# Start of the second phase of a fused network kernel: rows moved inside SBUF in eight transfers, the last mixed tile in halves, the weight sums divided

## What is computed

```python
def ffn0(x):              # both operands rounded to float8 by one scale for the whole tensor
    amax = max(abs(x)); inv = amax / 448
    return (fp8(x / inv) @ fp8(w.T / w_inv)) * inv * w_inv + bias
mixed = einsum('boi,bih->boh', agg_w, x) + agg_b     # agg_w, agg_b from a small network of cond
x = x + ffn0(mixed)
conv = grouped_conv1d(x, weight, taps=9, groups=4) + ctx + fside   # over the 1024 positions
x = x + conv @ dequantised(W_q).T + bias
```

## Time and profile before

| | |
|---|---|
| median of 3 runs | 534.8 us (534.0 to 535.83) |
| profiled execution, its time | 535.84 us |
| its span, first to last instruction | 534.0 us |
| mean granted TensorE clock | 0.99 |
| TensorE busy in matmuls | 512.7 us (96%) |
| VectorE, ScalarE, GpSimd busy | 411.8, 245.6, 56.4 us |

### The profile page before, as it was taken

How to read it: one execution, slowest core, us unless ns; L and a number is a source line. 1 busy time by engine, 2 the same in 40 slices (tenths; PEclk the granted TensorE clock), 3 DMA queues, 4 the chain that set the end, 5 groups by cost and what they waited for, 6 DMA issues and landing times.

```text
span 534.0 us, 9541 instructions
## 1 busy us (share of the span) xinstructions
PE 512.7 (96%) x3526; PEld 286.5 (54%) x3526; DVE 411.8 (77%) x518; ACT 245.6 (46%) x286; POOL 56.4 (11%) x59
## 2 busy tenths in 40 slices
PE   4999999869999999999999999999999999999997
PEld 3644444336555555555555555555555555555563
DVE  4789999884888777777777777777777777777652
ACT  3488897654544444444444444444444444442310
POOL 6257775000000000000000000000000000000000
PEclk9999999889999999999999999999999999999999
DMA  6999491144666655656665655665555555566632
GB/s 190 398 390 401 148 354 61 44 154 126 182 197 202 188 179 178 178 178 178 180 180 181 185 186 185 186 180 178 178 178 178 178 178 178 180 185 188 198 120 79
DMA packets 86347, 101.28 MB, mean 190 GB/s; under 512 B 34156, under 2 KB 67694, under 8 KB 86334
## 3 DMA queue, kind: packets, MB, share of 16 engines
q1 hardware_dynamic: 85770, 100.89, 59.3%
q10 hardware_dynamic: 372, 0.20, 0.1%
q0 software_dynamic: 192, 0.02, 0.0%
HBM read 59.47 MB, written 33.82 MB: 175 GB/s over the span
## 4 chain that ended last, share of the span: by engine, by line
PE 82%; DVE 10%; POOL 2%; issue 2%; DMA 1%; ACT 1%; DVEq 0%; POOLq 0%; ACTq 0%
PE pair L1107 41%; PE pair L1085 19%; PE pair L1097 16%; DVE stat L759 5%; PE pair L995 2%; PE pair L1075 1%; DVE work L691 1%; PE pair L983 1%; DVE work L774 1%; DMA work<-split_rows 1%; DVE work L694 1%; DVE Y L774 1%; POOL work L436 1%; POOL Y L449 1%; POOL fixed L469 1%
## 5 line engine op out<-in xcount | busy, mean ns | idle before, releaser
L1107 PE MATMUL pair<-f1T,work 128*128 128x512 f16 x1024 | 231.0, 379 | 0.0
L1107 PEld LDWEIGHTS pair<-f1T,work 128*128 128x128 f16 x1024 | 98.9, 98 | 113.5
L580 ACT ACTIVATE work<-Y,consts 128x1024 bf16 (+1 forms) x29 | 33.3, 1148 | 186.9 <-DVE work L848 186.9
L867 DVE TENSOR_TENSOR work<-Y,work 128x512 f16<-128x512 f16 (+1 forms) x64 | 71.1, 1118 | 46.4 <-ACT work L609 45.2
L1085 PE MATMUL pair<-f0T,work 128*128 128x512 bf16 x464 | 104.9, 379 | 0.0
L1097 PEld LDWEIGHTS pair<-taps,work 128*128 128x128 f16 x1536 | 90.2, 99 | 9.5 <-issue 2.2
L1097 PE MATMUL pair<-taps,work 128*128 128x128 f16 x1536 | 92.7, 221 | 1.9 <-DMA work<-split_rows 1.9
L880 DVE TENSOR_TENSOR Y<-pair,Y 128x512 f32 (+1 forms) x64 | 44.0, 687 | 43.9 <-PE pair L1107 43.9
L609 ACT CAST work<-Y 128x512 f16 (+1 forms) x64 | 69.6, 1138 | 15.6 <-DVE Y L857 15.6
L1085 PEld LDWEIGHTS pair<-f0T,work 128*128 128x128 bf16 x464 | 45.4, 98 | 54.7
L995 PE MATMUL pair<-Y,work 128*128 128x512 f32 x128 | 62.7, 625 | 1.1 <-ACT Y L553 0.8
(11 more groups left out here) (149 smaller groups left out, 234.7 us busy)
## 6 DMA issues: line engine op xcount, KB each, us to landing
Y<-in_x_dram SPq DMA_DIRECT2D x64, 512.0 KB, 3.8
split_rows<-work SPq DMA_DIRECT2D x32, 520.0 KB, 2.6
work<-split_rows SPq DMA_DIRECT2D x32, 520.0 KB, 3.9
out_dram<-Y SPq DMA_DIRECT2D x31, 512.0 KB, 3.7
Y<-in_L_ffn_weight_dram SPq DMA_DIRECT2D x8, 512.0 KB, 5.9
Y<-in_L_ffn_W_q_dram SPq DMA_DIRECT2D x5, 512.0 KB, 14.0
work<-in_L_ffn_W_q_dram SPq DMA_DIRECT2D x3, 512.0 KB, 15.3
out_dram<-Y SPq DMA_DIRECT2D x2, 256.0 KB, 2.0
```

The source lines that it names most:

```text
L867: nc.vector.tensor_tensor(split[:, r, s, 1], v[:, r, :], split[:, r, s, 0], ALU.subtract)\
L1107: last = mm(ps[2 + h][:, :], y1s[n][:, e, k, :], f1T[:, k, h * H:(h + 1) * H], start=False, stop=(e == 1 and k == KT - 1), skip_group_chec ...
```

## The change

For tiles 0 and 1, `turn` is replaced by transfers within SBUF. For each of the eight groups one DMA takes sixteen partitions of `split` (4160 bytes each) straight to 128 partitions of `convin` (520 bytes each). SP issues groups 0 and 1 of each half b, and the GpSimd queue groups 2 and 3. The convolution waits for each half by itself, on `moved_sp[b]` and `moved_pool[b]`. For tile 1 the moves wait for conv(0)'s half b, and `hi(1)` waits for the moves of tile 0. From tile 2 on the way over DRAM stays, with its counts shifted.

The last mixed tile is stored and searched in halves. Three of the eight products of `weight_sums(0)` go between the transpose of the exchange and its broadcast. `fixed_parts` falls into a fixed and a sum part, placed between other work. Tile 2's transposes use PSUM banks 6 and 7, and are written as h = 0 and h = 1. On VectorE `first_quantise(2)` goes ahead of `residual0(1)`. ScalarE's loop has its first two steps written out.

```diff
@@ -172,6 +172,7 @@
...
         groups += [(25, 2), (27, 2), (29, 1), (30, 1), (31, 1)]
+        groups[-1:] = [(31, 0), (31, 1)]
         NGRP = len(groups)
@@ -273,6 +274,8 @@
...
         lo_done = sem("lo_done")
+        moved_sp = [sem(f"moved_sp{b}") for b in range(NB)]
+        moved_pool = [sem(f"moved_pool{b}") for b in range(NB)]
         split_out = sem("split_out")
@@ -295,6 +298,12 @@
...
             return turn_order.index((kind, n))
+        def split_row(g):
+            return split[g * CG:(g + 1) * CG].rearrange("p r s e -> p (r s e)")
+        def conv_row(g):
+            return convin[:, g].rearrange("p s e -> p (s e)")
@@ -379,7 +388,7 @@
...
             def turn(t, n, conv_read):
-                both, back = held(sp, 2 * t + 2), held(sp, 16 * t + 16)
+                both, back = held(sp, 2 * t + 2), held(sp, 16 * t - 16)
                 if conv_read is not None:
@@ -393,10 +402,19 @@
...
                 load_x(t, t % 2)
-            turn(0, 0, None)
+            def move(t):
+                sp.wait_ge(lo_done, 2 * t + 2)
+                for b in range(NB):
+                    if t:
+                        sp.wait_ge(conv_done, b + 1)
+                    for g in (b * G, b * G + 1):
+                        sp.dma_start(conv_row(g), split_row(g)).then_inc(moved_sp[b], 16)
+            move(0)
             sp.wait_ge(first_q, 6)
             load_x(2, 0)
-            turn(1, 1, 2)
+            move(1)
             sp.wait_ge(f0_done, 4)
@@ -503,6 +521,14 @@
...
+            for t in range(2):
+                pool.wait_ge(lo_done, 2 * t + 2)
+                for b in range(NB):
+                    if t:
+                        pool.wait_ge(conv_done, b + 1)
+                    for g in (b * G + 2, b * G + 3):
+                        pool.dma_start(conv_row(g), split_row(g)).then_inc(moved_pool[b], 16)
@@ -549,9 +575,11 @@
...
-                act.wait_ge(mixed, t + 1)
-                nc.scalar.activation(slot(t), pair[t % 2][:, :], ACT.Identity, bias=aggcol[:, t:t + 1])\
-                    .then_inc(mixed_ev, 1)
+                for h in range(2 if t == T - 1 else 1):
+                    c = slice(h * H, (h + 1) * H) if t == T - 1 else slice(0, L)
+                    act.wait_ge(mixed, t + 1 + h)
+                    nc.scalar.activation(slot(t)[:, c], pair[t % 2][:, c], ACT.Identity, bias=aggcol[:, t:t + 1])\
+                        .then_inc(mixed_ev, 1)
@@ -591,7 +619,7 @@
...
-                pb = ps[4 + h][:, 0:H // 2].bitcast(bf16).rearrange("p (k m) -> p k m", k=KT // 2)
+                pb = ps[(6 if t == 2 else 4) + h][:, 0:H // 2].bitcast(bf16).rearrange("p (k m) -> p k m", k=KT // 2)
                 act.wait_ge(q_turned, 2 * t + h + 1)
@@ -603,8 +631,12 @@
...
                 for h in range(2):
-                    if h == 0:
-                        act.wait_ge(split_out, 16 * t)
+                    if h == 0 and isinstance(t, int) and t < 3:
+                        for b in range(NB if t else 0):
+                            act.wait_ge(moved_sp[b], 32 * t)
+                            act.wait_ge(moved_pool[b], 32 * t)
+                    elif h == 0:
+                        act.wait_ge(split_out, 16 * t - 32)
                     r = slice(4 * h, 4 * h + 4)
@@ -674,11 +706,17 @@
...
             scaled(3)
-            with act.Fori(2, T - 2 - 1, 2) as i:
+            def loop_step(t, n):
+                scaled(t + 2, n)
+                hi(t)
+                yhi(t - 1, 1 - n)
+            loop_step(2, 0)
+            loop_step(3, 1)
+            with act.Fori(4, T - 2 - 1, 2) as i:
                 for n in range(2):
-                    scaled(i + n + 2, n)
-                    hi(i + n)
-                    yhi(i + n - 1, 1 - n)
+                    loop_step(i + n, n)
             hi(T - 2)
@@ -755,8 +793,13 @@
...
                 t, k = groups[n]
-                dve.wait_ge(mixed_ev, t + k)
-                nc.vector.tensor_reduce(stat[:, n:n + 1], slot(t, k), AX.X, ALU.max,
+                if t < T - 1:
+                    dve.wait_ge(mixed_ev, t + k)
+                    part = slot(t, k)
+                else:
+                    dve.wait_ge(mixed_ev, T + k)
+                    part = slot(t)[:, k * H:(k + 1) * H]
+                nc.vector.tensor_reduce(stat[:, n:n + 1], part, AX.X, ALU.max,
                                         apply_absolute_value=True).then_inc(mixed_red, 1)
@@ -896,8 +939,8 @@
...
             lo(0)
+            first_quantise(2)
             residual0(1, 1, 16)
-            first_quantise(2)
             dve.wait_ge(fixed_ev, 4)
@@ -994,10 +1037,11 @@
...
                               start=True, stop=True)
+                    if h or t == T - 1:
+                        last.then_inc(mixed, 1)
                     if t == 1 and h == 0:
...
                         nc.tensor.transpose(ps[7][0:1, 0:P], w_part, ident[:, :]).then_inc(w_pe, 1)
-                last.then_inc(mixed, 1)
@@ -1050,17 +1094,18 @@
...
                     turned1(turns1[t])
-            def turned_first_q(t):
-                for h in range(2):
-                    pb = ps[4 + h][:, 0:H // 2].bitcast(bf16)
-                    pe.wait_ge(first_q, 2 * t + h + 1)
-                    if t:
-                        pe.wait_ge(qT_in[1 - t % 2], 8 * h + 8)
-                    for k in range(4):
-                        at = (4 * h + k) * P
-                        last = nc.tensor.transpose(pb[:, k * P:(k + 1) * P], qn[t % 2][:, at:at + P], ident_b)
-                    last.then_inc(q_turned, 1)
+            def turned_first_q(t, h):
+                pb = ps[(6 if t == 2 else 4) + h][:, 0:H // 2].bitcast(bf16)
+                pe.wait_ge(first_q, 2 * t + h + 1)
+                if t == 1:
+                    pe.wait_ge(qT_in[0], 8 * h + 8)
+                if t == 2:
+                    pe.wait_ge(fixed_ev, 2 * h + 2)
+                for k in range(4):
+                    at = (4 * h + k) * P
+                    last = nc.tensor.transpose(pb[:, k * P:(k + 1) * P], qn[t % 2][:, at:at + P], ident_b)
+                last.then_inc(q_turned, 1)
@@ -1087,8 +1132,12 @@
...
             def conv(t, first=False):
-                pe.wait_ge(split_in, 16 * t + 16)
+                if not (isinstance(t, int) and t < 2):
+                    pe.wait_ge(split_in, 16 * t - 16)
                 for b in range(NB):
+                    if isinstance(t, int) and t < 2:
+                        pe.wait_ge(moved_sp[b], 32 * t + 32)
+                        pe.wait_ge(moved_pool[b], 32 * t + 32)
                     if not first:
@@ -1108,43 +1157,54 @@
...
-            def weight_sums(h):
+            def weight_sums(h, ks):
                 c = slice(h * H, (h + 1) * H)
-                for k in range(KT):
+                for k in ks:
                     last = mm(ps[h][0:NS, :], windowc[:, 3 * (R8 - 1 - k):3 * (R8 - 1 - k) + NS], f1T[:, k, c],
                               start=(k == 0), stop=(k == KT - 1))
-                last.then_inc(shifted_mm, 1)
-            def fixed_parts(h):
-                c = slice(h * H, (h + 1) * H)
+                if ks[-1] == KT - 1:
+                    last.then_inc(shifted_mm, 1)
+            def fixed_part(h):
                 pe.wait_ge(shifted_ev, h + 1)
-                mm(ps[2 + h][:, :], combT[:, 0:P], shifted[:, c], start=True, stop=True).then_inc(fixed_mm, 1)
-                mm(ps[6 + h][:, :], combT[:, P:2 * P], shifted[:, c], start=True, stop=True).then_inc(wsum_mm, 1)
+                mm(ps[2 + h][:, :], combT[:, 0:P], shifted[:, h * H:(h + 1) * H], start=True, stop=True)\
+                    .then_inc(fixed_mm, 1)
+            def wsum_part(h):
+                mm(ps[6 + h][:, :], combT[:, P:2 * P], shifted[:, h * H:(h + 1) * H], start=True, stop=True)\
+                    .then_inc(wsum_mm, 1)
...
             pe.wait_ge(mixed_ev, T - 1)
-            weight_sums(0)
+            weight_sums(0, range(0, 5))
             pe.wait_ge(mixed_red, NGRP + 1)
             nc.tensor.transpose(ps[7][0:1, 0:P], part_max, ident[:, :]).then_inc(x_pe, 1)
+            weight_sums(0, range(5, KT))
             pe.wait_ge(mixed_red, NGRP + 2)
             mm(ps[7][:, 128:129], ones, x_all, start=True, stop=True).then_inc(x_pe, 1)
-            weight_sums(1)
+            weight_sums(1, range(KT))
             pe.wait_ge(tapsum_made, 1)
             pe.wait_ge(ld["b0"], 32)
-            pe.wait_ge(mixed_ev, T)
-            fixed_parts(0)
-            turned_first_q(0)
+            pe.wait_ge(mixed_ev, T + 1)
+            fixed_part(0)
+            turned_first_q(0, 0)
+            wsum_part(0)
+            turned_first_q(0, 1)
             first_ffn0(0, 0, 0)
-            turned_first_q(1)
+            turned_first_q(1, 0)
+            turned_first_q(1, 1)
+            fixed_part(1)
             first_ffn0(1, 1, 0)
-            fixed_parts(1)
-            turned_first_q(2)
+            pe.wait_ge(x_step, 4)
```

(4 more changed lines are left out.)

## The result

The changed kernel takes 533.88 us (median of 20 runs, 532.73 to 535.26) against 534.89 us for the kernel before, also over 20 runs (533.67 to 536.34). The ratio is 0.9978, with a 95% interval of 0.9968 to 0.9987. That is 1.0 us gained where 3.85 were forecast: the right sign, but within the 0.3% that I had called no change, and above the top of the range (533.4).

The account below looks back on a forecast made before the run. TensorE, busy for 96% of the span and alone from 123.16 us on, bounds the kernel, so only an earlier start gains. Terms -0.2 - 3.45 - 0.2 = -3.85 us take the 534.8 median to 531.0, range 528.9 to 533.4.

Parts of the forecast that it names:

- Last tile in halves: Tile 31's reduction ahead of the exchange: gain 0.37 us, 0.2 given back by three products before the broadcast, net -0.2.
- Fixed part 1 moved: Ahead of the first layer of tile 1: that layer ends 0.4 us late, which costs nothing.
- What is late next: Before conv(0): tile 2's transposes, not the moves, set its start, at 115.1 instead of 118.56, -3.45 us.
- The moves: Behind lo(0): 2.1 us from issue to landing, half 0 there at 114.5 and half 1 at 115.6, before conv(0) needs them.
- My second rival: Moves of tile 0: sixteen partitions feed a transfer slowly, conv(0) starts 2.8 us earlier, 531.7 us; chance 0.10.
- conv(0): The first convolution: takes 4.4 us instead of 4.60 as the clock falls soon after its start, -0.2; bounds 2.68 and 5.4.
- The third rival: Half 0's moves: GpSimd's descriptors wait for VectorE, conv(0) gains only 1.5 us, 533.0 to 533.2 us; chance 0.16.
- GpSimd's transfers didn't run one after the other: Slower rival at conv(1): GpSimd's transfers run in series, 538.6 us if each takes 2.5 us; chance 0.10.
- The clock didn't stay high: Rival at conv(0): the clock stays high and it takes 2.68 us, 529.2 us in all; chance 0.18.

Follow-up runs that it names:

- experiment 4: The changed kernel with all eight products of weight_sums(0) ahead of the exchange: 532.93 us, ratio 0.9948 to the kernel before.
- Experiments 2: The changed kernel with SP moving groups 0 and 2 of each half and GpSimd 1 and 3: 531.22 us, ratio 0.9941 to the kernel before.
- 5: The changed kernel with half 0's four moves on GpSimd's queue and half 1's on SP's: 533.09 us, ratio 0.9969 to the kernel before.
- 8: The changed kernel with all eight moves on SP's queue and none on GpSimd's: 532.54 us in a single run.
- Experiment 3: The changed kernel with 14 idle products into a free PSUM bank ahead of conv(0): 531.76 us, ratio 0.9926 to the kernel before.

## Why the prediction was wrong

**Last tile in halves: right.** Forecast -0.37 and +0.2, net -0.2; measured -0.53 and +0.31, net -0.22. That the net fits so well is partly luck, as both parts came out larger: a half took 0.60 us and not 0.68, and the broadcast slipped by the most that I had allowed. The three products cost what they last beyond the 0.37 us gap, as experiment 4 shows from the other side.

**Fixed part 1 moved: right.** It costs nothing. The first layer of tile 1 ends near 110.1, and residual0(1) comes at 112.4.

**What is late next: half right.** Tile 2's transposes stand where the forecast put them (3.25 us after lo(0) against 3.26). first_quantise(2) took 2.89 us beside four GpSimd issues, 2.88 without them. But they don't set the start of conv(0).

**The moves: the step that failed.** I let half 0 land 2.64 us after lo(0), and it took 5.4. The price of one transfer was nearly right (2.1 forecast, 2.3 and 2.5 measured alone). Wrong was to price eight as one plus the issues ahead of it. First, SP's issue of this shape takes 0.6 us and not 0.34; I had read that price from a transfer of another shape. That alone is 0.3 us for the second one. Second, and more, transfers of two queues at once held each other up, to 2.7 to 4.7 us. My second rival came nearest to the mechanism, and its data phase was about right (4.8 us for eight; here the DMA engines worked on them for 4.2, from 111.0 to 115.2), but it let half 0 finish in half of that. It doesn't: half 1's transfers run beside half 0's, and SP's second one, which half 0 needs, landed after 4.7. Experiments 2, 5 and 8 each thin the crowd in another way and bring conv(0) to 4.6, 5.0 and 4.8 us.

**conv(0): the second step that failed**, -0.2 forecast and +0.7 measured. I had counted on a gap of 2 us ahead of conv(0). It was 2.3 behind the last transposes and 3.7 with only 0.4 us of work in it, the clock fell before conv(0), and it ran low almost to its end. My upper bound of 5.4 was right. The term hung on the moves. Whether the clock would have held with conv(0) at 3.3 us, no run shows: the earliest start, 4.6 us after lo(0), had the clock low from 113.5 as well. Experiment 3 shows its size, 2.4 us.

With the two terms as measured my sum reads -0.2 - 1.2 + 0.7 = -0.7, against -1.0 in the medians.

**Two sums.** By its own terms the lower end of my range is 529.0, not 528.9. The third rival with the sum's other terms is 532.9, not 533.0 to 533.2, which would put the upper end near 533.1. Neither changes that 533.9 lies outside.

**The rivals.** GpSimd's descriptors didn't wait for VectorE: its four issues took 2.13 us together, 0.53 each, all of them beside VectorE's first_quantise(2). The rule of the Trainium skill that I had named there (page "SBUF — State Buffer", section "SBUF: two separate sides") changed nothing here. It speaks of VectorE's two-port modes, and no row shows in which mode these operations ran. GpSimd's transfers didn't run one after the other either. The clock didn't stay high.

**Reading a single profile.** The profiled executions differ by 2.6 us, and 1.5 of it is the first layer of tile 0, which the change doesn't touch. Taken as the change's own, it would have seemed to confirm most of my sum.

**Open.** Why half 0 of eight well dealt moves needs 4.6 us, and all eight 6.5, where one takes 2.5 wasn't separated further: neither the order within a queue nor the size of a transfer was varied alone, and with this dealing tile 2's load was also issued 1.2 us sooner (112.60 against 113.81), beside the last moves. That the instruction packet delays the load is read from two kernels that have both, and wasn't tried alone.

## What to carry to other kernels

Price a crowd of transfers as a crowd: take issue and landing from a transfer of the same shape, run one alone and then the whole set, and try dealing those that run at the same time to partitions 16 or 64 apart instead of 32 (here 0.9 and 0.5 us for the first half, nothing for the last transfer at 16). Before TensorE's start is moved forward, look at what the gap ahead of it does to the clock; here idle products in the gap (2.4 us) were worth more than the shorter way (1.2 us). And where executions fall into groups by mean granted clock, compare within a group before a microsecond is given to an edit, and look in a profile which low stretches make up the group, as the edit may have removed one of them.

## What the runs showed of the hardware

- A move of 65 KB from 16 to 128 partitions within SBUF landed after 2.5 us on SP and 2.3 on GpSimd, one of the same size from 128 to 128 after 1.9. SP's issue took 0.6 to 0.68 us for the narrow shape and 0.55 for the wide one.
- Two queues at once, reading 32 partitions apart: SP's second landing 4.5 to 4.8 us in five profiles (3.6 in a sixth, where the queues started 0.6 us apart), SP's issues up to 1.23 us. Reading 16 apart: 3.8 to 3.9 in three profiles, the four SP issues at 0.60 to 0.67 each, conv(0) 0.9 us sooner, but the last of the eight no sooner (6.5 us after lo(0) against 6.1).
- Fourteen idle products ahead of conv(0) kept the granted clock at 1.00 where it had been 0.50: conv(0) took 2.84 us instead of 5.27, and the kernel 2.5 us less in both groups of runs.
- Five idle products at a place where nobody waited for them went with 1.4 to 1.9 us more at the same mean clock (534.65 us at 0.994, against 532.8 to 533.2 for the changed kernel), together with a tile's load that landed after 5.4 us instead of 3.3 and a 0.02 MB instruction packet beside it.
